# Twelve FFN units over one token half first, score products of step 0 ahead of natural(1), and context keys 2 and 3 expanded in one go

## The chip, the cores and the metric

The kernel runs on one core of one Trainium2 chip. The time is the device time of one execution in microseconds (us), the median of several runs. The core has five engines with queues of their own: TensorE (PE in the profile), VectorE (DVE), ScalarE (ACT), GpSimd (POOL) and SyncE (SP), which here only issues DMA. Each engine works its list of instructions in order and waits on semaphores.

## The reference

One transformer layer on x of 4 batches x 256 tokens x 128 channels, with a context of 4 x 64 tokens x 64 channels:

```python
h  = layernorm(x)
q, k, v  = heads(h @ Wq + bq), heads(h @ Wk + bk), heads(h @ Wv + bv)   # 16 heads of 8
qc = heads(h @ Wcq + bcq);  kc, vc = heads(ctx @ Wck + bck), heads(ctx @ Wcv + bcv)
y  = softmax(causal(q k^T / sqrt(8))) v + softmax(qc kc^T / sqrt(8)) vc
x1 = x + y @ Wp + bp
h2 = layernorm(x1)
aff = sigmoid(h2 @ Wr + br)                  # 32 experts; the top 8, scaled to sum 1, give w_full
shared = (silu(h2 @ Wg_s + bg_s) * (h2 @ Wu_s + bu_s)) @ Wd_s + bd_s
down_e = (silu(h2 @ Wg[e] + bg[e]) * (h2 @ Wu[e] + bu[e])) @ Wd[e] + bd[e]   # inner size 64
out = x1 + shared + sum_e w_full[:, e] * down_e
```

All 32 experts are computed for all 1,024 tokens and weighted afterwards.

## The kernel before

**Precision.** Nearly every operand x is held as a rounded half `x_hi` and a rest `x_lo = x - x_hi`, and a product is three matmuls: hi*hi, hi*lo, lo*hi (`product3`, lines 1341 to 1343). ACT makes the rounded half, DVE or POOL the rest, so each product has two small steps on other engines in front of it.

**Attention.** 16 steps (`STEPS`), step i being batch i // 4 and head group i % 4 (4 heads). PE's loop (line 1603) does in step i: the first two score products (`scores(i, 0)`, `scores(i, 1)`), the transposes of the row maxima of step i+1 (`turn_max`), the natural scores of step i+2 for those maxima (`natural`, with `turn_out(i - 2)` inside), the last two score products (`scores(i, 2)`, `scores(i, 3)`), whatever `tail_at[i]` lists, then the value products of step i-1 (`attend_self`, `attend_context`), then `late_at[i]`. DVE builds key blocks (`expand`), takes the maxima (`maxima`) and divides the outputs (`normalize`); ACT places the maxima (`shift`), takes exponentials (`exps`), rounds and copies (`copy_out`); POOL applies the causal selection to probs, builds context key blocks of groups 2 and 3 (`expand_ctx`, line 592), adds self and context outputs (`add_y`) and makes the rests of FFN weights (`split_unit`, line 626). In step 0 PE also does `natural(1)` before the loop and `context_values` between the score products.

**The tail of a batch.** When the 4 steps of a batch are done: `y_turn` (transpose), `project` (product with Wp; DVE adds x, takes `stats`; POOL raises to the power -0.5; DVE `norm`), `x2_turn` (transpose), `router` (product with Wr; ACT sigmoid or Silu; DVE `top`, `weights`), `route_turn` (transpose). Each goes through PSUM bank 7 (`B_MISC`), and `take_misc` makes PE wait until the one before has been read. For batches 0 and 1 these lie between attention steps (`tail_at`, `late_at`, `between_at`), for batches 2 and 3 partly beside the FFN: the tables `pe_beside`, `act_beside`, `v_beside` (lines 334 to 358) say at which item n and in which of three places (A, B, C) each engine takes them.

**FFN.** 17 units (`UNITS`): 16 pairs of experts, and the shared one. Tokens come in two halves of 512 (`CHUNK`); half 0 is batches 0 and 1, half 1 is batches 2 and 3. One item is one unit over one half; `WORK` (line 53) lists the 34 items: the first `LEAD` = 6 units over half 0, the same 6 over half 1, then units one by one over both halves, and the last 4 units over half 0 and then half 1. Item n on PE: gate (3 matmuls), place A, up (3), place B, wide (1, the routing weights spread over rows, `spread_routes`), down of item n-2 (3), place C. ACT takes Silu of gate and rounds hid, DVE computes `gated` and `hid`, and the rest `hid_lo` is made by POOL for the items in `POOL_LO` (0 to 7 and 31) and by DVE for the others. The first gate over half 1 is item 6 and needs `x2_turn` of batch 3; its wide needs `route_turn` of batch 3. Attention and FFN share PSUM banks: wide 1 waits for `normalized` 15 (line 1664).

**Weights.** SP loads each unit into one of 6 slots (`load_unit`), a load of unit u waits until POOL has made the rest of unit u-6. ACT rounds (`round_unit`, line 799), for units from 6 on after item `SPLIT_AT` and after PE's last down of the unit that had the slot, since rounded half and rest have 6 slots too.

## Time and profile before

| | us |
|---|---|
| median of 3 runs | 215.67 |
| the three runs | 212.80, 215.67, 219.47 |
| the profiled execution | 214.26 |
| its span, first to last instruction | 212.5 |
| PE busy | 192.5 (91%) |
| DVE busy | 161.1 (76%) |
| ACT busy | 136.0 (64%) |
| POOL busy | 95.7 (45%) |

The profiled execution took 214.26 us, 1.76 more than its span. The page gives the busy time of each engine, the busy share and the clock granted to TensorE in 40 slices, the chain of work that ended last (70% PE, 12% DVE, 6% issue, 5% ACT, 3% POOL), and the costliest groups of instructions. Times below are from the start of the span. In rows of the timeline the bracket at the end is the idle time of the engine before the instruction and what released it.

### The profile page before, as it was taken

What the parts mean: (1) busy time and instruction counts of PE and PEld (TensorE: products, weight loads), DVE (VectorE), ACT (ScalarE), POOL (GpSimd) and SP (SyncE); (2) the same over time, 40 slices, a digit from 0 to 9 for tenths busy, and PEclk for the clock granted to TensorE, in tenths of its full rate; (3) what the DMA queues carried; (4) which work ended last, traced back from release to release, by engine and by line L of the source; (5) the groups of instructions that cost most, each with busy time, mean ns of one, the idle gap of its engine ahead of it and who ended that gap; (6) DMA issues with size and microseconds to landing.
All of it is one profiled execution on the core that took longest, in us unless ns stands there. A gap on an engine that the chain in (4) does not pass through costs nothing.

```text
span 212.5 us, 4008 instructions
## 1 busy us (share of the span) xinstructions
PE 192.5 (91%) x1249; PEld 140.5 (66%) x1249; DVE 161.1 (76%) x379; ACT 136.0 (64%) x272; POOL 95.7 (45%) x150
## 2 busy tenths in 40 slices
PE   7967979999999996999797886949999999999993
PEld 2635757777777674777565664737888888887662
DVE  2989997676788869985731689776778888887882
ACT  4456778787898886897735444424577566555571
POOL 7799782142644766277342152516254332220020
PEclk9999999999999999999958999999999999999999
DMA  4365423232333242103101010000033000000003
GB/s 114 87 150 141 108 65 79 55 81 71 93 96 79 69 103 57 37 0 77 37 3 37 0 37 2 0 0 3 0 75 78 19 2 0 0 0 0 5 0 99
DMA packets 20434, 10.40 MB, mean 49 GB/s; under 512 B 11881, under 2 KB 18542, under 8 KB 20414
## 3 DMA queue, kind: packets, MB, share of 16 engines
q1 hardware_dynamic: 19290, 9.24, 17.6%
q0 software_dynamic: 672, 0.69, 1.4%
q10 hardware_dynamic: 452, 0.23, 0.5%
q8 instruction: 10, 0.16, 0.3%
q14 instruction: 10, 0.08, 0.1%
HBM read 4.51 MB, written 0.52 MB: 24 GB/s over the span
## 4 chain that ended last, share of the span: by engine, by line
PE 70%; DVE 12%; issue 6%; ACT 5%; POOL 3%; DMA 1%; POOLq 1%; DVEq 0%; ACTq 0%
PE psum L1341 12%; PE psum L1342 11%; PE psum L1343 10%; PE psum L1444 5%; PE psum L1535 4%; PE psum L1523 4%; PE psum L1500 4%; PE psum L1443 3%; PE psum L1547 3%; PE psum L1667 3%; PE psum L1505 3%; PE psum L1466 2%; PE psum L1528 2%; PE psum L1509 2%; PE psum L1486 1%
## 5 line engine op out<-in xcount | busy, mean ns | idle before, releaser
L913 ACT ACTIVATE gate<-psum,bias_cols 128x512 f32<-128x512 f32 (+2 forms) x35 | 23.5, 675 | 28.7 <-PE psum L1343 28.6
L790 ACT ACTIVATE probs<-psum 128x512 f32<-128x512 f32 x64 | 36.4, 597 | 7.3 <-PE psum L1505 3.4
L1285 DVE SCALAR_TENSOR_TENSOR gated<-psum,bias_cols,gate 128x512 f32<-128x512 f32 x32 | 24.0, 750 | 11.5 <-ACT gate L913 11.5
L629 POOL TENSOR_TENSOR w_ffn_lo<-w_ffn,w_ffn_hi 128x384 fp32r<-128x384 f32 x17 | 20.6, 1212 | 26.7 <-ACT w_ffn_hi L804 26.0
L1341 PE MATMUL psum<-xT_hi,w_ffn_hi 128*128 128x512 f32 x66 | 26.9, 407 | 0.0
L1342 PE MATMUL psum<-xT_lo,w_ffn_hi 128*128 128x512 f32 x66 | 26.1, 396 | 0.0
L1343 PE MATMUL psum<-xT_hi,w_ffn_lo 128*128 128x512 f32 x66 | 26.0, 393 | 0.0
L1444 PE MATMUL psum<-key_blocks,query_rows 96*128 96x512 f32 x48 | 24.1, 544 | 0.0
L699 POOL TENSOR_TENSOR hid_lo<-hid,hid_hi 128x512 fp32r<-128x512 f32 x9 | 11.6, 1291 | 25.9 <-ACT hid_hi L922 25.1
L1297 DVE TENSOR_TENSOR hid<-gated,psum 128x512 f32<-128x512 f32 x32 | 21.8, 682 | 1.6 <-PE psum L1667 1.1
L922 ACT CAST hid_hi<-hid 128x512 fp32r<-128x512 f32 (+1 forms) x33 | 20.2, 613 | 3.8 <-DVE hid L1297 3.1
L654 POOL TENSOR_SCALAR_AFFINE_SELECT probs<-probs 128x512 f32<-128x512 f32 x16 | 10.3, 643 | 22.9 <-ACT probs L790 22.9
L1080 DVE TENSOR_REDUCE row_max<-psum 128x4 fp32r<-128x1024 f32 x16 | 19.5, 1216 | 0.0
L962 DVE TENSOR_TENSOR hid_lo<-hid,hid_hi 128x512 fp32r<-128x512 f32 (+2 forms) x26 | 17.2, 663 | 1.1 <-ACT hid_hi L922 0.9
L797 ACT COPY o_sb<-psum 128x512 f32<-128x512 f32 x16 | 9.4, 586 | 11.7 <-PE psum L1535 11.7
L658 POOL TENSOR_SCALAR_AFFINE_SELECT probs<-probs 128x512 f32<-128x512 f32 x16 | 10.2, 637 | 14.2 <-ACT probs L790 14.2
L1076 DVE TENSOR_REDUCE row_max<-psum 128x4 fp32r<-128x512 f32 x16 | 11.0, 689 | 6.8 <-PE psum L1444 6.8
L1443 PE MATMUL psum<-causal,ident_bf 128*128 128x512 bf16 x32 | 12.5, 389 | 3.4 <-DVE key_blocks L982 1.7
L728 ACT ACTIVATE key_blocks<-key_rows,head_mask 100x256 fp32r<-100x256 f32 x32 | 14.4, 498 | 1.3 <-DMA key_rows<-keys 1.3
L1341 PE MATMUL psum<-hid_hi,w_ffn_hi 128*128 128x512 f32 (+2 forms) x35 | 14.4, 411 | 0.4 <-POOL hid_lo L699 0.3
L1343 PEld LDWEIGHTS psum<-xT_hi,w_ffn_lo 128*128 128x128 f32 x66 | 12.5, 189 | 3.1
L1341 PEld LDWEIGHTS psum<-xT_hi,w_ffn_hi 128*128 128x128 f32 x66 | 12.4, 188 | 3.1 <-issue 0.6
(184 smaller groups left out, 476.5 us busy)
## 6 DMA issues: line engine op xcount, KB each, us to landing
query_rows<-queries SPq DMA_DIRECT2D x46, 64.0 KB, 2.1
key_rows<-keys SPq DMA_DIRECT2D x39, 32.0 KB, 1.9
w_ffn<-in_L_ffn_Wg SPq DMA_DIRECT2D x16, 64.0 KB, 1.9
w_ffn<-in_L_ffn_Wu SPq DMA_DIRECT2D x16, 64.0 KB, 2.2
w_ffn<-in_L_ffn_Wd SPq DMA_DIRECT2D x16, 64.0 KB, 2.1
ckey_rows<-ckeys POOLq DMA_DIRECT2D x12, 32.0 KB, 1.9
key_rows<-keys POOLq DMA_DIRECT2D x9, 32.0 KB, 1.8
x_sb<-in_x SPq DMA_DIRECT2D x2, 128.0 KB, 2.6
```

The lines of the kernel that those rows point to most:

```text
L629: ins = pool.tensor_tensor(w_ffn_lo[:, k, :, :], w_ffn[:, k, :, :], w_ffn_hi[:, k, :, :].bitcast(F32), ALU.subtract).then_inc(ffn_lo, 1)
L790: act.activation(probs[:, i % 2, c, :], bank(B_ST + c % 2), ACT.Exp, scale=SCALE).then_inc(exp_done, 1)
L913: act.activation(gate[rows_of(n), n % 3, part], psum[of, B_GATE + n % 2, part], ACT.Silu, bias=bias_cols[of, BIAS_GATE + u:BIAS_GATE + u + ...
L922: act.copy(hid_hi[rows_of(n - 1), (n - 1) % 3, :], hid[rows_of(n - 1), (n - 1) % 3, :]).then_inc(hid_rounded, 1)
L1080: dve.tensor_reduce(to[:, 1, :], psum[:, B_NAT1:B_NAT1 + 2, :].rearrange("p k (j c) -> p j k c", j=GROUP), AX.XY, ALU.max).then_inc(max_do ...
L1285: dve.scalar_tensor_tensor(out=gated[:, n % 3, :], in0=bank(B_UP + n % 2), scalar=bias_cols[:, BIAS_UP + u:BIAS_UP + u + 1], in1=gate[:, n ...
L1297: dve.tensor_tensor(hid[:, n % 3, :], gated[:, n % 3, :], bank(B_WIDE + n % 2), ALU.mult).then_inc(hid_done, 1)
L1341: pe.matmul(dst, w_hi, x_hi, start=start, stop=False, skip_group_check=True)
L1342: pe.matmul(dst, w_hi, x_lo, start=False, stop=False, skip_group_check=True)
L1343: return pe.matmul(dst, w_lo, x_hi, start=False, stop=stop, skip_group_check=True)
L1443: pe.matmul(to, ident_bf[:, :], causal[:, :, :], start=True, stop=False, skip_group_check=True)
L1444: return pe.matmul(to, query_rows[0:KR, b % 2, g, 0, P * q:P * (q + 1)], blocks[:, :, P * k:P * (k + 1)], start=not diagonal, stop=True, s ...
```

## The change

1. `LEAD` is 12: twelve units go over half 0, then the same twelve over half 1. `POOL_LO` becomes items 0 to 11 and 31. The number of matmuls does not change.
2. Units 6 to 16 get places of their own for the rounded half and the rest (`w_late_hi`, `w_late_lo`), so rounding no longer waits for a down; ACT rounds them after items 2 to 7, 14, 16, 18, 20 and 22 (`ROUND_AT`), and POOL splits units 6 to 11 between its `lower_half` calls.
3. The tail of batches 2 and 3 is laid out anew over items 0 to 10. `x2_turn(2)` leaves step 15 for item 0; `attend(15)` and `turn_out(14)` go behind up of item 0, `turn_out(15)` behind up of item 1. `route_turn(1)` is now ahead of the FFN on ACT too.
4. The transposed outputs of steps 12 to 15 go to banks 0, 1, 3 and 6 instead of the shared bank 7 or 5, with waits on `normalized` in front of gate 0, gate 1 and up 1.
5. In steps 13 to 15 DVE puts the sigmoid rest of `router(1)` behind `y_turn(2)`, and `weights(1)` behind `normalize(12)`; in step 15 PE does `turn_out(13)` ahead of `attend(14)`. POOL takes the power of batch 2 after its loop.
6. Step 0: PE does `scores(0, 0)` and `scores(0, 1)` ahead of `natural(1)`, and `scores(0, 2)`, `scores(0, 3)` ahead of `turn_max(1)`; ACT and DVE are reordered to suit; POOL expands context keys 2 and 3 in one go, ahead of the first selection.

```diff
-LEAD = 6
+LEAD = 12
-SPLIT_AT = {LAST_USE[u - SLOTS] + 4: u for u in range(SLOTS, UNITS)}
+ROUND_AT = {n: u for n, u in zip((2, 3, 4, 5, 6, 7, 14, 16, 18, 20, 22), range(SLOTS, UNITS))}
...
+        w_late_hi = sb("w_late_hi", [P, UNITS - SLOTS, 3, P], F32R)
+        w_late_lo = sb("w_late_lo", [P, UNITS - SLOTS, 3, P], F32R)
...
-        between_at[STEPS - 1] = [("norm", 2)]
-        tail_at[STEPS - 1] = [("x2_turn", 2), ("route_turn", 1)]
+        tail_at[STEPS - 1] = [("route_turn", 1)]
+        pe_beside = {(0, "B"): [("attend", STEPS - 1), ("turn_out", STEPS - 2)],
+                     (0, "C"): [("x2_turn", 2)],
+                     (1, "B"): [("turn_out", STEPS - 1)],
+                     (1, "C"): [("router", 2)],
+                     (2, "C"): [("y_turn", 3)],
+                     (3, "C"): [("project", 3)],
+                     (5, "C"): [("route_turn", 2), ("x2_turn", 3)],
+                     (6, "C"): [("router", 3)],
+                     (LEAD - 2, "B"): [("route_turn", 3)]}
+        act_beside = {(0, "B"): [("x2_turn", 2)],
+                      (2, "B"): [("router", 2)],
+                      (3, "A"): [("y_turn", 3)],
+                      (5, "C"): [("route_turn", 2), ("x2_turn", 3)],
+                      (7, "B"): [("router", 3)],
+                      (LEAD - 2, "B"): [("route_turn", 3)]}
+        v_beside = {(0, "C"): [("turn_out", STEPS - 2), ("x2_turn", 2)],
+                    (1, "C"): [("turn_out", STEPS - 1), ("router", 2)],
+                    (2, "C"): [("top", 2)],
+                    (3, "A"): [("y_turn", 3)],
+                    (3, "C"): [("project", 3), ("stats", 3)],
+                    (4, "A"): [("weights", 2)],
+                    (4, "C"): [("norm", 3)],
+                    (6, "A"): [("x2_turn", 3)],
+                    (6, "C"): [("router", 3)],
+                    (7, "C"): [("top", 3)],
+                    (8, "C"): [("weights", 3)]}
+        RSTD_ITEM = 4
-        POOL_LO = [*range(8), LAST_ITEM - 2]
+        POOL_LO = [*range(LEAD), LAST_ITEM - 2]
...
-            return {STEPS - 2: B_ST + 1, STEPS - 1: B_OUT}.get(i, B_MISC)
+            return {STEPS - 4: B_NAT0, STEPS - 3: B_NATC, STEPS - 2: B_NAT1 + 1, STEPS - 1: B_OUT}.get(i, B_MISC)
...
             expand_ctx(2)
-            pool.wait_ge(pool_ckey_blocks_set, GROUP)
+            expand_ctx(3)
+            pool.wait_ge(pool_ckey_blocks_set, 2 * GROUP)
...
+            tail("project", 2)
+            split_unit(SLOTS - 1)
             add_y(STEPS - 2)
-            add_y(STEPS - 1)
-            split_unit(SLOTS - 1)
...
                 if n == RSTD_ITEM:
                     tail("project", BATCH - 1)
+                if n == 1:
+                    add_y(STEPS - 1)
                 lower_half(n)
-            for u in range(SLOTS, UNITS):
+                if n + 1 in ROUND_AT:
+                    split_unit(ROUND_AT[n + 1])
+            for u in range(LEAD, UNITS):
                 split_unit(u)
...
-                if u >= SLOTS:
-                    act.wait_ge(m_down, LAST_USE[u - SLOTS] + 1)
-                act.copy(w_ffn_hi[:, k, :, :], w_ffn[:, k, :, :]).then_inc(ffn_rounded, 1)
+                act.copy(hi_of(u), w_ffn[:, k, :, :]).then_inc(ffn_rounded, 1)
...
+            exps(0, (0, 1))
             expand(2)
+            act.wait_ge(have_neg_mean, 1)
+            norm(4)
+            norm(5)
+            exps(0, (2, 3))
+            shift(1)
+            norm(6)
+            norm(7)
...
             expand_ctx(1)
+            expand(2)
             maxima(1)
-            expand(2)
             cvalues()
...
             turn_max(0)
-            natural(1)
             for i in range(STEPS):
...
                 scores(i, 0)
                 scores(i, 1)
                 if i == 0:
+                    natural(1)
                     context_values()
+                    scores(0, 2)
+                    scores(0, 3)
...
                 pe.wait_ge(ffn_lo, u + 1)
+                if n < 2:
+                    pe.wait_ge(normalized, STEPS - 3 + n)
...
+                        if n == 1:
+                            pe.wait_ge(normalized, STEPS - 1)
```

## Rows read from the trace of the kernel before

**Rows 1.** Busy time by stretch: each engine's us and instructions, granted clock, DMA
```profile
142.00:200.00 58.00, 58.00 (x250) 46.24 (x250) 45.66 (x70) 34.63 (x62) 18.47 (x14) 1.00 0.07 16
```
**Rows 2.** Timeline of PE, 101 to 142 us, instructions behind a stall
```profile
103.75 0.63 PE L1547 MATMUL psum<-ident,o_sb 128*128 128x128 f32 x4 [0.43 <-DVE yT_lo L962]
...
105.96 0.33 PE L1341 MATMUL psum<-w_qkv_hi,yT_hi 128*128 128x128 f32 x1 [0.90 <-DVE o_norm L1115]
...
114.40 0.44 PE L1596 MATMUL psum<-ident,route 128*128 128x128 f32 x2 [1.10 <-DVE xT_lo L962]
...
118.41 0.28 PE L1341 MATMUL psum<-w_r_hi,xT_hi 128*128 128x32 f32 x1 [0.95 <-ACT routeT L824]
...
126.32 0.30 PE L1341 MATMUL psum<-w_qkv_hi,yT_hi 128*128 128x128 f32 x1 [0.74 <-DVE yT_lo L962]
...
132.52 0.41 PE L1584 MATMUL psum<-ident,x_norm 128*128 128x128 f32 x2 [1.39 <-DVE x_norm L1183]
...
141.84 0.41 PE L1596 MATMUL psum<-ident,route 128*128 128x128 f32 x2 [2.70 <-DVE route L1203]
```
**Rows 3.** Busy time by stretch: where the granted clock is low
```profile
106.00:113.40 7.40, 7.30 (x42) 5.03 (x42) 2.48 (x10) 2.94 (x6) 2.97 (x6) 0.54 0.09 19
```
**Rows 4.** Timeline of PE in steps 0 and 1, behind a stall
```profile
20.08 0.38 PE L1443 MATMUL psum<-causal,ident_bf 128*128 128x512 bf16 x1 [1.40 <-issue]
...
30.33 0.50 PE L1466 MATMUL psum<-ckey_blocks,query_rows 96*128 96x256 f32 x2 [1.07 <-POOL ckey_blocks L597]
```
**Rows 5.** Timelines of POOL and DVE, 22 to 31 us
```profile
27.85 2.42 POOL L597 TENSOR_TENSOR ckey_blocks<-ckey_rows,head_mask 100x256 fp32r<-100x256 f32 x4
...
23.07 1.24 DVE L982 TENSOR_SCALAR key_blocks<-key_rows,head_mask 100x256 fp32r<-100x256 f32 x2
...
26.98 1.22 DVE L1080 TENSOR_REDUCE row_max<-psum 128x4 fp32r<-128x1024 f32 x1
```
**Rows 6.** Busy time by stretch: gate 0, attend(15), turn_out(14); and two score products
```profile
114.60:117.25 2.65, 2.65 (x29) 1.38 (x28) 0.00 (x0) 1.12 (x3) 0.00 (x0) 1.00 0.00 0
104.14:104.95 0.81, 0.81 (x9) 0.72 (x6) 0.71 (x3) 0.08 (x2) 0.30 (x1) 1.00 0.00 0
```
**Rows 7.** Timeline of ACT, 104 to 118 us
```profile
104.87 1.08 ACT L790 ACTIVATE probs<-psum 128x512 f32<-128x512 f32 x2 [0.73 <-PE psum L1505]
...
108.87 0.51 ACT L804 CAST w_ffn_hi<-w_ffn 128x384 fp32r<-128x384 f32 x1
...
113.90 1.28 ACT L898 ACT_TABLE_LOAD   x1
...
117.40 0.69 ACT L913 ACTIVATE gate<-psum,bias_cols 128x512 f32<-128x512 f32 x1
```
**Rows 8.** The page's costliest groups: count, busy us and mean ns, idle before
```profile
L1285 DVE SCALAR_TENSOR_TENSOR gated<-psum,bias_cols,gate 128x512 f32<-128x512 f32 x32 | 24.0, 750 | 11.5 <-ACT gate L913 11.5
...
L1297 DVE TENSOR_TENSOR hid<-gated,psum 128x512 f32<-128x512 f32 x32 | 21.8, 682 | 1.6 <-PE psum L1667 1.1
L922 ACT CAST hid_hi<-hid 128x512 fp32r<-128x512 f32 (+1 forms) x33 | 20.2, 613 | 3.8 <-DVE hid L1297 3.1
...
L797 ACT COPY o_sb<-psum 128x512 f32<-128x512 f32 x16 | 9.4, 586 | 11.7 <-PE psum L1535 11.7
```
**Rows 9.** Groups of instructions on POOL, 142 to 200 us, same columns
```profile
L629 POOL TENSOR_TENSOR w_ffn_lo<-w_ffn,w_ffn_hi 128x384 fp32r<-128x384 f32 x11 | 14.6, 1326 | 26.0 <-ACT w_ffn_hi L804 26.0
L699 POOL TENSOR_TENSOR hid_lo<-hid,hid_hi 128x512 fp32r<-128x512 f32 x3 | 3.9, 1293 | 6.1 <-ACT hid_hi L922 6.1
```
**Rows 10.** Timelines of DVE and POOL, 117 to 132 us
```profile
117.79 0.29 DVE L1115 TENSOR_TENSOR o_norm<-psum,r_den 128x128 f32<-128x128 f32 x1
...
123.34 1.18 DVE L1187 TENSOR_TENSOR affinity<-exp_neg,r_logits 128x64 f32<-128x64 f32 x1
...
131.77 0.60 DVE L1183 TENSOR_SCALAR x_norm<-x,moments,rstd 128x128 f32<-128x128 f32 x2 [0.16 <-POOL rstd L646]
...
131.03 0.71 POOL L646 TENSOR_TENSOR rstd<-var_eps,minus_half 128x2 f32<-128x2 f32 x1 [3.12 <-DVE var_eps L958]
```

More of the change, by code:

```diff
@@ L329, in build @@
         tail_at[STEPS - 2] = [("project", 2)]
-        between_at[STEPS - 1] = [("norm", 2)]
-        tail_at[STEPS - 1] = [("x2_turn", 2), ("route_turn", 1)]
-        pe_beside = {(0, "A"): [("attend", STEPS - 1), ("turn_out", STEPS - 2), ("router", 2)],
-                     (0, "B"): [("turn_out", STEPS - 1)],
-                     (1, "B"): [("y_turn", 3)],
-                     (2, "C"): [("project", 3)],
-                     (3, "C"): [("route_turn", 2)],
-                     (4, "A"): [("x2_turn", 3)],
-                     (4, "C"): [("router", 3)],
-                     (LEAD, "B"): [("route_turn", 3)]}
@@ L915, in _ @@
                 if n == 0:
-                    tail("route_turn", 1)
+                    copy_out(STEPS - 1)
                 left_over(n, "A")
@@ L1228, in _ @@
                     maxima(i + 2, i - 2)
-                else:
-                    if i == STEPS - 2:
-                        long_part("weights", 1)
-                    for name, b in between_at.get(i, ()):
-                        long_part(name, b)
-                    normalize(i - 2)
+                if i == STEPS - 2:
+                    tail_rest("router", 1)
+                    normalize(i - 2)
+                    long_part("weights", 1)
+                if i == STEPS - 1:
+                    normalize(i - 2)
+                    long_part("norm", 2)
+                    break
                 for name, b in tail_at.get(i, ()):
```

87 lines of the change are left out of this document (32 added, 55 removed).

## The prediction

> **What bounds the kernel now.** I read the page's engine totals first: PE is busy for 91% of the span and has 70% of the chain that ended last, so the question is where PE does not work, or works slowly. Then the busy time by stretch. From 142 to 200 us PE is never idle and issues 250 matmuls in 58.0 us [rows 1]: 0.232 us each, 2.32 us for an item of ten. DVE has 45.7 us there, ACT 34.6, POOL 18.5. This stretch is bound by the number of matmuls, and the change leaves that number alone. So only what lies ahead of it can move. From 101 to 142 us, the end of attention and the first seven items, the timeline of PE shows eight stalls over 0.4 us [rows 2] (seven stand there; the eighth is 0.45 us, at 130.00): 0.43, 0.90, 1.10, 0.95, 0.74, 0.45, 1.39 and 2.70, in sum 8.66 us. All are waits for DVE or ACT in the tail of batches 2 and 3. The reader should see from the releasers that this is one chain: six items (14 us of PE) are too little cover for what follows attention(15), and the chain's last link, `route_turn(3)`, stands in PE's queue ahead of item 6. The row of the granted clock shows one more loss there: between 106.0 and 113.4 it is 0.54 on average though PE is busy for 7.30 of 7.40 us [rows 3], so most of it ran at 1.2 GHz instead of 2.4. That is (1 - 0.54) x 7.4 = 3.4 us lost, and it follows the stalls of 0.43 and 0.90. At the start, `natural(1)` comes after 1.40 us without work, and `natural(3)` waits 1.07 us for POOL's context keys [rows 4].
>
> **Step 0.** Before, PE waits 1.40 us for key blocks of step 1 while the shift that `scores(0, 0)` needs is nearly there. The two score products now fill that gap, and `natural(1)` starts when it did. The reductions of step 1 start 0.3 us later (DVE now does `expand(2)` first), but the expansion of step 2 that took 1.24 us beside POOL's work is out of their way. What sets `turn_max(2)` is DVE's last reduction of step 2, ending at 28.20 [rows 5]. Walking DVE's list with these durations I get 27.9, since its `expand(3)` now meets POOL and takes the 1.24. That is 0.3 us. POOL's second expansion, 2.42 us starting at 27.85, now follows the first at about 24.8 and ends at 27.2, so `natural(3)` at about 28.3 doesn't wait: 1.07 us more, with its restart 1.2. The selection of step 0 moves from 25.5 to 27.2 and ends at 28.5; its reader `attend(0)` comes at about 31. Key rows and query rows issued by SP are landed well before either order asks. Sum 1.5 us. Bounds: nothing, if DVE's chain sets everything; 2.5, both stalls whole. From 30 to 101 us PE is full but for one wait in step 10 that the change leaves, so I take the gain as lasting.
>
> **Steps 13 to 15.** `turn_out(12)` has a bank of its own, so it no longer waits until `y_turn(2)` is read (0.43). `project(2)` no longer waits for `normalize(12)` (0.90). `x2_turn(2)` leaves the queue, and with it the 1.10 wait of `route_turn(1)`, which now only needs `weights(1)`, long ready. PE has little idle time left there, and I expect the clock to stay at 2.4 GHz: 3.4 us. POOL now takes the rest of unit 4 ahead of the selection of step 15, and waits with it for ACT's rounding; both are done before `attend(15)`, which stands behind gate 0 and up 0. Then the 0.95 behind `routeT` goes, because `router(2)` is an item later.
>
> **A new stall in item 1.** Up 1 writes the bank of `turn_out(14)` and waits for `normalize(14)`, which on DVE stands behind gated 0 and hid 0, and these behind the first Silu. Count from the end of `attend(14)`. PE: two score products 0.81; `route_turn(1)` 0.2; gate 0, `attend(15)`, `turn_out(14)` 2.65 [rows 6]; up 0 0.70; wide 0 0.23; `x2_turn(2)` 0.2; gate 1 0.70: 5.5 us. ACT: copy 0.59 [rows 8], rounding 0.51, two exponentials 1.08, routeT 0.4, table load 1.28 and its dummy 0.2, Silu 0.69 [rows 7]: 4.75; DVE: gated 0.75, hid 0.68 [rows 8], normalize 0.55 (its second half is 0.29, [rows 10]): 6.75. PE waits 1.3 us. The ends are nothing and 2.5 (if the chain starts a microsecond later). Before, the table load lay beside idle PE time. The Trainium skill (ScalarE: Activation LUTs, Terms) says about 2.7 us for a table load, and in its section What ACT_TABLE_LOAD costs about 1.28; the trace agrees with the second, and by the first this stall would be 2.7 us.
>
> **Items 2 to 11.** Now twelve items, 28 us, lie over the tail of batch 3, and every other wait of rows 2 (0.74, 0.45, 1.39, 2.70) belongs to a link which now has at least one item of slack, but one: `x2_turn(3)` behind item 5. From the end of gate 4: ACT Silu 0.69 and hid 0.61 [rows 7, 8]; POOL rest of hid 1.29, the split of unit 8 1.33 [rows 9], the power 0.71, then DVE's norm 0.60 [rows 10]: 5.2, with hand-overs 5.4. PE: up 4, wide, down 2, all of item 5 and `route_turn(2)`: 4.3. A new stall of 1.1 us; nothing to 2.5. `lower_half(4)` waits behind the same norm on POOL, down 4 is read 4.7 us after wide 4 and still in time. Per item POOL now has 1.29 + 1.33 = 2.62 us against PE's 2.32 in the six items with a split: it falls behind by 0.3 each, 1.8 in all, and the two items between hid and down cover that. Rounding costs ACT 0.51 in items where it has over 0.9 free. SP loads units 6 to 10 before the FFN as now; unit 11 is asked for at about 113 and rounded ten microseconds later.
>
> **The sum.** Removed 8.66 + 3.4 = 12.1; added 1.3 + 1.1 = 2.4; step 0 1.5; together 11.2 us. The profiled execution took 214.26 (span 212.5), so 203.1. The median of the three runs is 1.4 higher; I can't see why, part of it is likely a longer stretch at 1.2 GHz, so I carry half over: 203.8.
>
> **The rivals.**
> (a) Forecast: 203.8, its own range 201.5 to 206. Chance 0.60.
> (b) The clock falls again. The 1.3 us stall stands among transposes and value products with few rows or columns, as the 0.43 and 0.90 did before 106 us. Against it: stalls of 1.10 and 0.95 between such work, and 2.70 later, left the clock at 1.00. Price 3.4: 207.2. Chance 0.15.
> (c) DVE or POOL becomes the bound in items 2 to 8. DVE has 2.32 - 1.43 = 0.89 us free an item, 7.1 over eight, and both `top` and `weights` of two batches, which made the wait of 2.70, with stats and norms: some 11 us, as an estimate. It falls 3 to 4 us behind; the slack of up is about two items. And `affinity`, 64 elements, took 1.18 us while POOL made a rest [rows 10]; four such per batch could wait a POOL instruction each, 1.3 us. Then PE waits some 3 us: 206.8. Chance 0.13. The Trainium skill (SBUF — State Buffer, SBUF: two separate sides) says that DVE instructions with two SBUF inputs and POOL's exclude each other for a whole instruction; the trace agrees with that 1.18, and this rule speaks against a change that gives POOL four more rests beside the tail.
> (d) It gives little: the stalls only moved and the waits come back as others of the same chain, since `project(3)`, `x2_turn(3)` and `route_turn(2)` still need DVE in order. Kept: the clock's 3.4 and half of step 0: 211. Against it: 13 more FFN matmuls (3.0 us) now stand ahead of `y_turn(3)`, and five more items between it and `route_turn(3)`. Chance 0.09.
> (e) Slower. All of items 0 to 11 now hang on POOL's `hid_lo`. If POOL's 1.29 were stretched by DVE's lock, PE would run at POOL's pace. To eat 11 us in twelve items, POOL has to take 3.3 us an item; for slower by 2%, 3.7: 220. Rows 9 have 1.29 beside a DVE at 79%. Chance 0.03.
>
> **How the numbers follow.** The low end is the sum without the two new stalls, 200.7; the high end adds the clock (3.4), the whole 1.4 of the median and 0.6 of (c): 208.5. Beyond stand (d), (e) and a little of (c). Faster by over 2% (about what a measurement of this kernel can tell from no change) is below 211.4: (a), (b), (c) and half of (d), 0.93. Within 2%: 0.04. Slower: 0.03.
>
> **What would show it.** Right: PE's timeline from the last attention step to item 12 has two stalls over 0.5 us, before up 1 (releaser DVE `o_norm`) and before `x2_turn(3)` (DVE `x_norm`); granted clock 1.00 throughout; `y_turn(3)` at about 118, gate 0 at about 107; `natural(3)` without a wait. Wrong: stalls before downs with POOL `hid_lo` as releaser mean (c) or (e); before ups or wides with DVE `gated` or `hid`, (c); a clock near 0.5 between 105 and 120, (b). The early gain is wrong if PE's `scores(2, 0)` starts later than 33.

## The result, and the profile after

Four executions of the changed kernel took 204.82, 204.88, 205.11 and 206.95 us, median 205.0; the kernel before had a median of 215.1 beside them. The ratio is 0.9585, with a 95% interval of 0.9477 to 0.9693. (The ratios here and below leave out executions of over 1.5% above the fastest of the same kernel.) The prediction was 203.8, in a range of 200.5 to 208.5. The profiled execution took 204.82 (span 203.1), against 214.26 (span 212.5) before.

The timeline of PE after the change, the instructions behind a stall of over 0.2 us from 84 us to the end of the tail (start, us, engine, line, operation, then the idle time before it and its releaser; line numbers are 8 to 20 higher than before):

```profile
112.27 0.50 PE L1356 MATMUL psum<-xT_hi,w_ffn_hi 128*128 128x512 f32 x1 [1.01 <-DVE o_norm L1127]
...
120.15 0.30 PE L1356 MATMUL psum<-w_qkv_hi,yT_hi 128*128 128x128 f32 x1 [0.24 <-DVE yT_lo L974]
...
126.06 0.41 PE L1611 MATMUL psum<-ident,route 128*128 128x128 f32 x2 [0.35 <-DVE route L1215]
...
128.37 0.44 PE L1599 MATMUL psum<-ident,x_norm 128*128 128x128 f32 x2 [1.91 <-ACT routeT L834]
...
140.89 0.41 PE L1611 MATMUL psum<-ident,route 128*128 128x128 f32 x2 [0.74 <-DVE route L1215]
...
144.30 0.50 PE L1356 MATMUL psum<-hid_hi,w_late_hi 128*128 128x512 f32 x1 [0.47 <-POOL hid_lo L707]
```

These answer [rows 2]. They are up 1, `project(3)`, `route_turn(2)`, `x2_turn(3)`, `route_turn(3)` and down 9, and in sum 4.72 us where before there were 8.66. The prediction had two of them, 2.4 in sum.

Busy time by stretch after the change (us, then busy us and instruction count of PE, its weight load, DVE, ACT and POOL; the granted clock; DMA share and GB/s):

```profile
105.00:113.40 8.40, 7.39 (x60) 4.81 (x55) 4.50 (x14) 6.42 (x13) 5.30 (x8) 1.00 0.19 47
112.00:130.00 18.00, 15.22 (x74) 11.99 (x75) 15.90 (x41) 8.47 (x18) 10.93 (x12) 1.00 0.17 42
130.00:145.00 15.00, 13.79 (x63) 10.76 (x63) 13.38 (x29) 8.21 (x16) 9.70 (x9) 1.00 0.08 20
```

The first row answers [rows 3]: where the clock was 0.54 it is 1.00. The other two show who is full: DVE is busy for 29.3 of the 33 us from 112 to 145, 89%, and POOL for 20.6.

Steps 0 to 2 in PE's timeline, and the same queue at gate 0 and at `y_turn(3)`:

```profile
19.35 0.74 PE L1515 MATMUL psum<-query_rows,key_blocks 100*128 100x256 f32 x4 [0.76 <-DVE queries L1033]
20.00 0.38 PE L1458 MATMUL psum<-causal,ident_bf 128*128 128x512 bf16 x1
...
28.28 0.40 PE L1481 MATMUL psum<-ckey_blocks,query_rows 96*128 96x256 f32 x2
...
32.05 0.73 PE L1515 MATMUL psum<-query_rows,key_blocks 100*128 100x256 f32 x4
...
106.54 0.48 PE L1356 MATMUL psum<-xT_hi,w_ffn_hi 128*128 128x512 f32 x1
...
117.20 0.38 PE L1586 MATMUL psum<-ident,y_nat 128*128 128x128 f32 x2
```

`natural(1)` at 20.00 and the context part of `natural(3)` at 28.28 have no wait any more, against 1.40 and 1.07 in [rows 4]. Not all of the first gap is filled: `scores(0, 0)`, now ahead of `natural(1)`, waits 0.76 us for DVE. A wait of 0.30 at 24.40 in the kernel before is gone too, so the waits from 18 to 31 us fell from 2.77 to 0.76, by 2.0. `scores(2, 0)` starts at 32.05 (34.18 before), gate 0 at 106.54 (114.60 before), `y_turn(3)` at 117.20 (122.16 before).

**The clock, execution by execution.** Each execution comes with its mean granted clock, and the times go with it in steps. Executions of the two kernels, on the chips of these runs:

```
mean clock   kernel before, us        kernel after, us
0.997-0.999  none in 43               204.8, 204.9, 204.9, 205.0, 205.1
0.992        212.9 to 213.1           none
0.982-0.984  214.0 to 214.6           206.4, 206.5, 207.0
0.974-0.975  215.7 to 216.2           none
0.967        216.4 to 216.9           none
0.959        217.6 to 217.8           none
0.952        218.9 to 219.4           none
0.944        220.1 to 220.4           none
```

From 212.9 to 220.3 there are six steps, 1.2 us each on average. The kernel before was never seen at full clock; one step below 212.9 would be 211.7, an estimate, and an almost equal kernel (experiment 3) took 211.64 at 0.998. That gives 211.6. A second estimate comes from experiment 2, the kernel before with two banks changed, whose profiled execution was at 1.00 throughout. The first line of its page:

```profile
PE 189.3 (91%) x1249; PEld 138.5 (66%) x1249; DVE 161.3 (77%) x379; ACT 136.2 (65%) x272; POOL 95.9 (46%) x150
```

Its span was 208.5, so PE idled 19.2 us, 0.8 less than the 20.0 of the kernel before; 210.23 and 0.8 are 211.1. Profile to profile, the 9.4 us are then 2.7 to 3.2 for the clock and 6.2 to 6.7 at equal clock. The pages of the two kernels split them in another way: PE's idle time fell from 20.0 to 14.3 us, its busy time from 192.5 to 188.8, 5.7 and 3.7.

### The profile page after: what moved, and what is told of

Read it like the earlier page. It is cut to its first block, busy times and chain, and to the rows that moved or that the text cites. A ratio compares the mean times of both kernels' runs of the same rounds, so it can differ in the third digit from the quotient of the medians.

```text
span 203.1 us, 3982 instructions
## 1 busy us (share of the span) xinstructions
PE 188.8 (93%) x1237; PEld 138.5 (68%) x1249; DVE 162.2 (80%) x375; ACT 135.7 (67%) x272; POOL 98.1 (48%) x154
## 4 chain that ended last, share of the span: by engine, by line
PE 65%; DVE 18%; issue 6%; ACT 5%; POOL 3%; DMA 1%; DVEq 0%; POOLq 0%
PE psum L1356 10%; PE psum L1358 9%; PE psum L1357 9%; PE psum L1459 6%; PE psum L1515 5%; PE psum L1550 4%; PE psum L1538 4%; PE psum L1520 3%; PE psum L1562 3%; DVE gated L1300 2%; POOL hid_lo L707 2%; PE psum L1458 2%; PE psum L1687 2%; PE psum L1524 2%; PE psum L1543 2%
## 5 line engine op out<-in xcount | busy, mean ns | idle before, releaser
L707 POOL TENSOR_TENSOR hid_lo<-hid,hid_hi 128x512 fp32r<-128x512 f32 x13 | 16.8, 1291 | 32.9 <-ACT hid_hi L934 30.6
L638 POOL TENSOR_TENSOR w_late_lo<-w_ffn,w_late_hi 128x384 fp32r<-128x384 f32 x11 | 12.2, 1112 | 18.7 <-ACT w_late_hi L814 18.7
L1356 PE MATMUL psum<-xT_hi,w_late_hi 128*128 128x512 f32 x42 | 17.0, 404 | 0.0
L1358 PE MATMUL psum<-xT_hi,w_late_lo 128*128 128x512 f32 x42 | 16.6, 394 | 0.0
L1357 PE MATMUL psum<-xT_lo,w_late_hi 128*128 128x512 f32 x42 | 16.5, 392 | 0.0
L974 DVE TENSOR_TENSOR hid_lo<-hid,hid_hi 128x512 fp32r<-128x512 f32 (+2 forms) x22 | 15.2, 696 | 1.1 <-ACT hid_hi L934 0.9
L1687 PE MATMUL psum<-routeT,spread 128*128 128x512 f32 x32 | 12.8, 401 | 0.0
L1515 PE MATMUL psum<-query_rows,key_blocks 100*128 100x256 f32 x64 | 11.9, 307 | 0.8 <-DVE queries L1033 0.8
L1515 PEld LDWEIGHTS psum<-query_rows,key_blocks 100*128 100x128 f32 x64 | 8.6, 189 | 5.6 <-issue 4.4
L994 DVE TENSOR_SCALAR key_blocks<-key_rows,head_mask 100x256 fp32r<-100x256 f32 x32 | 11.9, 415 | 0.0
## 6 DMA issues: line engine op xcount, KB each, us to landing
x_sb<-in_x SPq DMA_DIRECT2D x2, 128.0 KB, 2.7
```

Of the source, the lines that this page charges most:

```text
L707: pool.tensor_tensor(hid_lo[:, n % 3, :], hid[:, n % 3, :], hid_hi[:, n % 3, :].bitcast(F32), ALU.subtract).then_inc(pool_lo_done, 1)
L1356: pe.matmul(dst, w_hi, x_hi, start=start, stop=False, skip_group_check=True)
L1357: pe.matmul(dst, w_hi, x_lo, start=False, stop=False, skip_group_check=True)
L1358: return pe.matmul(dst, w_lo, x_hi, start=False, stop=stop, skip_group_check=True)
L1515: ins = pe.matmul(psum[:, to, SEQ * j:SEQ * (j + 1)], key_blocks[0:ROWS, i % RING, 2 * c + j, 0:P], query_rows[0:ROWS, b % 2, g, 0, :], st ...
```

## The experiments

**1. How much step 0 gives, and whether it lasts.** The changed kernel with steps 0 to 2 and the spread of the context keys as before.

```diff
-            pool.wait_ge(pool_ckey_blocks_set, GROUP)
+            expand_ctx(3)
+            pool.wait_ge(pool_ckey_blocks_set, 2 * GROUP)
...
-            natural(1)
...
+                    natural(1)
...
+                    scores(0, 2)
+                    scores(0, 3)
```

(Here a plus is the changed kernel, which is undone; ACT's and DVE's lists go back with it.)

> The changed kernel with step 0 as in the kernel before: natural(1) ahead of the loop, the last two score products of step 0 behind natural(2), context keys 3 expanded behind the selections of step 0. Everything behind step 1 stays changed. In the two traces PE reaches scores(2, 0) 2.1 us earlier and y_turn(1) of step 10 still 2.1 us earlier after the change. Theory: the gain of step 0 lasts to the end, so this kernel takes 205.0 + 2.1 = 207.1 us and its PE stalls in the FFN stay at 4.7 us. Rival: the tail of the attention gives it back, 205.0 to 205.5. My prediction's term was 1.5 us.

Executions: 207.14 and 207.15 (clock 0.998, 0.991), 208.34 and 208.46 (0.990, 0.989); ratio to before 0.971 [0.965, 0.977]. PE's timeline of that kernel:

```profile
20.05 0.38 PE L1453 MATMUL psum<-causal,ident_bf 128*128 128x512 bf16 x1 [1.39 <-issue]
...
30.30 0.50 PE L1476 MATMUL psum<-ckey_blocks,query_rows 96*128 96x256 f32 x2 [1.07 <-POOL ckey_blocks L606]
...
132.04 0.44 PE L1594 MATMUL psum<-ident,x_norm 128*128 128x128 f32 x2 [1.90 <-ACT routeT L835]
```

Both early waits are back (and the 0.3 at 24.38) and every later wait over 0.3 us has the length that it has in the changed kernel (1.90 for 1.91, 0.74 for 0.74). At full clock it takes 207.1 against 204.9 to 205.0. So step 0 is worth 2.1 to 2.2 us, all of it reaches the end, and it doesn't touch the tail.

**2. The first two waits alone.** The kernel before, with a bank of its own for `turn_out` in steps 12 and 13.

```diff
-            return {STEPS - 2: B_ST + 1, STEPS - 1: B_OUT}.get(i, B_MISC)
+            return {STEPS - 4: B_NAT0, STEPS - 3: B_NATC, STEPS - 2: B_ST + 1, STEPS - 1: B_OUT}.get(i, B_MISC)
...
+                if n < 2:
+                    pe.wait_ge(normalized, STEPS - 3 + n)
```

> The kernel before, with one part of the change alone: the transposed outputs of steps 12 and 13 go to banks 0 and 1, with the waits this needs ahead of gate 0 and gate 1. Takes away what makes PE wait 0.43 us ahead of turn_out(12) and 0.90 us ahead of project(2). Theory (the clock fell because PE was idle there): the granted clock stays at 1.00 between 105 and 115 us, and the time falls by 1.3 for the waits and 3.4 for the clock, 215.1 to 210.4 us. Rival (the clock falls by itself in this stretch, where the work is transposes and value products): only 1.3 us, 213.8, with a stretch near 0.5 in the trace. Second rival: the waits come back at x2_turn(2) and route_turn(1), and nothing is gained.

Executions: 210.23 (1.0), 211.84 and 212.01 (0.991, 0.992), 214.62 (0.976); ratio 0.988 [0.980, 0.996]. PE's timeline in place of the first two rows of [rows 2]:

```profile
109.26 0.41 PE L1584 MATMUL psum<-ident,x_norm 128*128 128x128 f32 x2 [0.55 <-DVE x_norm L1183]
...
110.59 0.44 PE L1596 MATMUL psum<-ident,route 128*128 128x128 f32 x2 [0.92 <-DVE xT_lo L962]
```

The waits of 0.43 and 0.90 are gone, and 0.55 of a new one has come before `x2_turn(2)`. `route_turn(1)` waits 0.92 for 1.10, so the waits fell by 1.0 in all. At the same clock (0.991 to 0.992) this kernel takes 211.9 where the one before takes 212.9, which is that 1.0. Its median gained 2.6 against before; the rest came with the clock, which was 1.00 throughout in its profile. That execution fits the theory's 210.4; in the other three the clock fell all the same, so the two waits are not the only cause.

**3. The clock alone.** The kernel before, with four idle matmuls of the kernel's own kind ahead of `project(2)`. They add work that nothing reads and fill most of the wait of 0.90.

```diff
+                if i == STEPS - 2:
+                    run_idle(4, B_NAT0)
```

> The kernel before with four more matmuls of 512 columns into bank 0, which nothing reads, between the last score product of step 14 and project(2): 0.93 us of PE work where PE waits 0.90 us. No wait and no order of the rest is changed. Theory (idle time let the clock fall): granted clock 1.00 from 106 to 113 us, time lower by 3.4, about 211.7 us. Rival (the kind of work lets it fall, or the 0.43 alone is enough): clock 0.5 as before, time equal or up to 0.2 longer, 215.

Ten executions: 211.64 (0.998), 212.74 (0.992), three of 214.2 to 214.6 (0.984), 215.67 (0.976), four of 216.7 to 216.9 (0.967); ratio 0.999 [0.992, 1.006]. Busy time by stretch in its profile:

```profile
105.00:113.40 8.40, 7.14 (x68) 4.23 (x65) 3.61 (x15) 5.84 (x11) 4.10 (x7) 1.00 0.11 25
...
138.00:145.00 7.00, 5.94 (x20) 4.80 (x21) 3.60 (x8) 2.09 (x4) 2.58 (x2) 0.76 0.00 0
```

The clock held where the wait was filled, and fell behind the later wait of 2.69 (`route_turn(3)`), whose like of 2.70 in the profile of the kernel before had left it at 1.00. So the idea that this one gap makes the clock fall doesn't hold over many executions: with it filled, the clock falls elsewhere, and the median doesn't move.

**4. What POOL's instructions do to DVE's small ones.** The kernel before, with two subtractions of 128x512 on POOL behind `hid_lo(4)`, beside the work that feeds `route_turn(3)`. They are added work that nothing reads.

```diff
+                if n == 4:
+                    for k in range(2):
+                        pool.tensor_tensor(dump[:, k, :], x_sb[:, 0:4, :].rearrange("p t c -> p (t c)"),
+                                           x_sb[:, 4:8, :].rearrange("p t c -> p (t c)"), ALU.subtract)
```

> The kernel before with two more subtractions on POOL behind the rest of hid 4, 128x512, both inputs in SBUF, into a tile that nothing reads. They run at about 139 to 141.5 us, where POOL is idle and DVE does top(3) and weights(3), which took 1.36 us from 140.25 on. POOL's next work comes at 143. Theory (DVE's small instructions wait for a POOL instruction): weights(3) takes 1.2 to 2.5 us longer, some of its instructions measure about 1 us instead of 0.2, and the stall of PE ahead of route_turn(3), 2.70 us, becomes 4 to 5. Rival (1.18 us for affinity and the like come from something else, such as the Silu beside it): weights(3) stays at 1.4 us and the stall at 2.7.

Its one execution took 218.48 us at 0.969, a single time from which nothing is read. The timelines of POOL, DVE and PE in it:

```profile
140.74 2.50 POOL L709 TENSOR_TENSOR dump<-x_sb 128x512 f32<-128x512 f32 x2
...
142.34 0.98 DVE L1196 SCALAR_TENSOR_TENSOR affinity<-not_top,affinity 128x64 f32<-128x64 f32 x1
...
144.49 0.41 PE L1601 MATMUL psum<-ident,route 128*128 128x128 f32 x2 [3.42 <-DVE route L1208]
```

The twin of this `affinity` in the kernel before takes 0.23 us beside an idle POOL. Here it takes 0.98 and ends when POOL's pair ends (143.32 and 143.24). PE's wait grows by the same 0.7, from 2.70 to 3.42. The direction is confirmed; the size is less than I expected, since only one of the seven instructions of `weights(3)` fell into POOL's time.

**5. The stall of up 1.** The changed kernel, with DVE's normalization of step 14 ahead of the first gated product.

```diff
-        v_beside = {(0, "C"): [("turn_out", STEPS - 2), ("x2_turn", 2)],
+        v_beside = {(0, "A"): [("turn_out", STEPS - 2)],
+                    (0, "C"): [("x2_turn", 2)],
```

> The changed kernel with DVE's normalize(14) moved from behind hid 0 to ahead of gated 0. In the trace of after, turn_out(14) ended at 109.9 us, DVE waited until 110.18 for the first Silu, and up 1 waited 1.01 us for normalize(14). Theory: that stall goes, since normalize(14) no longer stands behind the Silu and the table load: minus 1.0 us, 204.0. Rival: the item is bound by the Silu anyway, hid 0 is 0.3 us later and the stall comes back as another ahead of up 2, wide 1 or down 0: 205.0.

Executions: 204.46 (0.991), 205.88 (0.983), 207.30 and 207.45 (0.974); ratio 0.959 [0.950, 0.968]. The wait ahead of up 1 is gone, those of 0.20, 0.35, 1.90 and 0.43 are as they were; the 0.74 ahead of `route_turn(3)` is missing as well, which experiment 9 explains by the clock. So the predicted mechanism holds. But the clock fell in all four executions, and the median, 206.6, gains nothing. At the same clock, 205.88 at 0.983 stands against 206.4 to 207.0 of the changed kernel, 0.6 to 1.1 less. In the profile it fell behind the waits at 80.8 (1.63) and at 128.8 (1.90), neither of which this edit touches.

**6. `x2_turn(3)` first.** The changed kernel, with `norm(3)` ahead of `weights(2)` on DVE and `x2_turn(3)` ahead of `route_turn(2)` on PE and ACT.

```diff
-                      (5, "C"): [("route_turn", 2), ("x2_turn", 3)],
+                      (5, "C"): [("x2_turn", 3), ("route_turn", 2)],
...
-                     (4, "A"): [("weights", 2)],
-                     (4, "C"): [("norm", 3)],
+                     (4, "C"): [("norm", 3), ("weights", 2)],
```

> The changed kernel with DVE's norm(3) ahead of weights(2) (weights(2) from ahead of gated 4 to behind norm(3)), and x2_turn(3) ahead of route_turn(2) on PE and ACT. In after, weights(2) took 3.1 us from 122.8 on, and gated 4, hid 4 and norm(3) followed it; PE waited 0.35 + 1.91 us behind item 5. Theory (DVE's queue made norm(3) late): norm(3) comes as soon as POOL's power is done, at 126.0 instead of 127.3, x2_turn(3) waits about 0.4 us, route_turn(2) waits for weights(2), done at about 129, some 1.5 to 2: gain between 0 and 1 us, 204.0 to 205.0, with x2_turn(3) a microsecond earlier. Rival, and what the prediction said (POOL's split of unit 8 sets it): x2_turn(3) isn't earlier.

Executions: 207.62 (0.991), 207.99, 208.35 and 209.06 (0.983); ratio 0.968 [0.961, 0.975]. PE's timeline:

```profile
126.67 0.41 PE L1598 MATMUL psum<-ident,x_norm 128*128 128x128 f32 x2 [1.10 <-DVE x_norm L1194]
...
130.84 0.69 PE L1610 MATMUL psum<-ident,route 128*128 128x128 f32 x2 [3.76 <-DVE xT_lo L973]
```

`x2_turn(3)` comes 1.7 us earlier, and 3.76 us of a new wait follow: `route_turn(2)` takes the same bank, and DVE reads `x2_turn(3)`'s out of it only in slot (6, A). An edit that I hadn't followed to the bank's next reader; what it shows is the first row.

**7. A longer lead.** The changed kernel with thirteen units over the first token half ahead instead of twelve, and unit 12 rounded after item 10.

```diff
-LEAD = 12
+LEAD = 13
-ROUND_AT = {n: u for n, u in zip((2, 3, 4, 5, 6, 7, 14, 16, 18, 20, 22), range(SLOTS, UNITS))}
+ROUND_AT = {n: u for n, u in zip((2, 3, 4, 5, 6, 7, 10, 16, 18, 20, 22), range(SLOTS, UNITS))}
```

> The changed kernel with thirteen units over half 0, so one item more of cover; route_turn(3) is at item 11, unit 12 is rounded after item 10, POOL makes the rests of items 0 to 12. Theory (the chain of batch 3 is still a little longer than its cover; DVE is late by then): the stall of 0.74 us ahead of route_turn(3) and the 0.47 behind it go, those at items 1 to 5 (3.5 us) stay: minus 1.0 us, 204.0. Rival (DVE is the bound over the whole stretch): the stalls move and the time stays 205.0.

Executions: 206.24 to 206.60 (0.991 to 0.983); ratio 0.959 [0.952, 0.966]. The 0.74 ahead of `route_turn(3)` is gone, the 0.45 ahead of down 9 stays, and so do 1.00, 0.36 and 1.91. But this profile was at 0.983, and there the changed kernel hasn't the 0.74 either (experiment 9), so it isn't shown that the edit removed it. At 0.983 it took 206.5 and 206.6 against the changed kernel's 206.4, 206.5 and 207.0: no gain can be told.

**8. Edits 5, 6 and 7 together.**

> The three edits together (normalize(14) ahead of gated 0, norm(3) ahead of weights(2), thirteen units first). Theory: they act on different stalls, the sum is minus 2.0 to 3.0: 202.0 to 203.0. Rival (DVE's whole work in items 0 to 8 is the bound): not below 204.

206.99 (0.992) to 209.20 (0.975); ratio 0.968 [0.960, 0.976]. Its waits are 0.24, 1.08, 3.76 and 0.43: those of experiment 6 without the ones that 5 and 7 remove. The 202.0 to 203.0 were missed by far, through the bank of experiment 6; nothing else can be read from it.

**9. The changed kernel once more,** on the chip and beside the kernels of experiments 10 and 11.

> The changed kernel itself, beside its variants on the same chip. So far four executions: 204.8, 204.9 and 205.1 us at a mean granted clock of 0.997 to 0.999, and 206.95 at 0.983. Variants with the same stalls of 1.91 and 0.35 us behind item 5 had a clock of 0.983 in most executions, with a stretch at half between 127 and 133 us, right behind those stalls. Theory: the clock also falls in this kernel in some executions, each time for 2 to 3 us of time: median 205.0 to 207.0. Rival: the changed kernel keeps its clock, 205.0 in nearly all.

204.92 and 204.99 (0.998), 206.44 and 206.48 (0.982); ratio 0.958 [0.950, 0.966]. The profiled one was at 0.982. Busy time by stretch of it, and `route_turn(3)` in PE's timeline:

```profile
80.00:84.00 4.00, 3.21 (x25) 1.48 (x26) 3.79 (x14) 1.23 (x3) 1.86 (x3) 0.67 0.46 113
...
127.00:133.00 6.00, 3.76 (x12) 2.97 (x13) 3.96 (x9) 3.02 (x7) 2.64 (x4) 0.72 0.16 36
...
142.60 0.39 PE L1611 MATMUL psum<-ident,route 128*128 128x128 f32 x2
```

The same two stretches of the first profile have 1.00 and 1.00. The waits that they follow are the same to 0.01 us in both: 1.65 at step 10, 1.91 ahead of `x2_turn(3)`. One program with the same waits thus kept its clock in one execution and lost it in another; it cost 1.5 us. Other waits are not the same: the 0.24 ahead of `project(3)` is gone, and so is the 0.74 ahead of `route_turn(3)`, where the slower PE comes later. The 0.74 is missing in every profile here with a low clock at 128 to 135 us (experiments 5 to 9). So such a profile can't show that an edit removed it.

**10. DVE's order mended for the bank.** The changed kernel, with `norm(3)` first, then the rest of `x2_turn(3)` in (5, B), `weights(2)` in (5, C), and `route_turn(2)` two items later.

```diff
-                      (5, "C"): [("route_turn", 2), ("x2_turn", 3)],
+                      (5, "C"): [("x2_turn", 3)],
+                      (7, "C"): [("route_turn", 2)],
...
-                     (4, "A"): [("weights", 2)],
-                     (6, "A"): [("x2_turn", 3)],
+                     (5, "B"): [("x2_turn", 3)],
+                     (5, "C"): [("weights", 2)],
```

> The changed kernel with another order on DVE in items 4 to 6: norm(3) right behind hid 4, the rest of x2_turn(3) between gated 5 and hid 5, and weights(2) only behind hid 5; route_turn(2), which needs weights(2), goes behind item 7 on PE and ahead of item 8's rounding on ACT. In after, norm(3) came at 127.31 us though POOL's power ended at 126.0, because weights(2) (3.1 us), gated 4 and hid 4 were ahead of it. Theory (DVE's queue, stretched by POOL's instructions, is what made x2_turn(3) late): the stalls of 0.35 and 1.91 us become one of 1.1 or less ahead of x2_turn(3), router(3) doesn't wait, and the clock no longer falls at 127 to 133 us: 1.2 to 2 us less than after at the same clock, 203.0 to 203.8. Rival (my prediction's: POOL's queue with the split of unit 8 sets norm(3)): x2_turn(3) at most 0.3 us earlier, 204.8. Second rival (DVE's whole work is the bound): the stall comes back ahead of an up, a wide or route_turn(3).

Executions: 204.97 to 205.24 (0.997 to 1.0, four), 206.49 and 206.69 (0.989, 0.988); ratio 0.957 [0.950, 0.965]. DVE's and PE's timelines:

```profile
126.08 0.60 DVE L1197 TENSOR_SCALAR x_norm<-x,moments,rstd 128x128 f32<-128x128 f32 x2 [1.69 <-POOL rstd L657]
...
126.83 0.41 PE L1601 MATMUL psum<-ident,x_norm 128*128 128x128 f32 x2 [1.09 <-DVE x_norm L1197]
...
133.66 0.44 PE L1613 MATMUL psum<-ident,route 128*128 128x128 f32 x2 [1.11 <-DVE logits L1158]
...
141.29 0.41 PE L1613 MATMUL psum<-ident,route 128*128 128x128 f32 x2 [0.83 <-DVE route L1217]
```

`x2_turn(3)` starts 1.5 us earlier, with DVE now idle for 1.69 until POOL's power is done. But the time at full clock is 205.0 as before: 1.11 has come ahead of `route_turn(2)` (its releaser is `logits`, DVE's reading of the bank), and the sum of the waits is 4.68 instead of 4.72. The forecast 203.0 to 203.8 was missed; the second rival held.

**11. Orders 10 and 5 together.** The diff is the two above.

> The order of e_order and normalize(14) ahead of gated 0. Each takes a stall of its own; the one ahead of up 1 (1.01 us) was gone in the trace of e_norm14. Theory: minus 1.0 for the one and 1.2 to 2 for the other, with a clock of 0.99 or more: 202.0 to 202.8 us. Rival: DVE is the bound over items 0 to 8, the sum isn't reached and the time stays above 203.5.

204.10, 204.12 and 204.17 (0.999, 1.0, 1.0), 205.41 to 205.74 (0.992 to 0.987); ratio 0.954 [0.947, 0.960]. The wait of up 1 is gone, the others stand (0.20, 1.09, 1.12, 0.83, 0.47). At full clock it is 0.8 us below the changed kernel (204.1 for 204.9) and 0.9 below experiment 10, from which it differs by this one edit: the 1.01 of up 1, nearly whole. The sum of the two gains wasn't reached, as the rival had it.

**12. Everything with slack.** As 11, with `route_turn(2)` at item 8 and `LEAD` 13.

> As e_both (normalize(14) ahead of gated 0, norm(3) and the rest of x2_turn(3) ahead of weights(2)), with route_turn(2) one place later (item 8, place B) and thirteen units over half 0, so that route_turn(3) is at item 11. e_both took 204.1 us in its three executions at a granted clock of 0.999 or more, with stalls of PE of 0.20, 1.09, 1.12 (ahead of route_turn(2)), 0.83 (ahead of route_turn(3)) and 0.47 us. Theory: DVE is late in items 6 to 9, and PE waits for it only where a link stands in PE's queue; with both links moved back the 1.12 and 0.83 go: 202.2 us at full clock. Rival (DVE's work, with its waits for POOL, is the bound up to item 10, wherever the links stand): ups, wides or downs wait instead, 203.5 to 204.1.

204.04 to 204.29 (1.0, three), 205.31 to 205.65 (0.992 to 0.987); ratio 0.950 [0.944, 0.955]. PE's timeline, in place of its last two links:

```profile
135.88 0.50 PE L1359 MATMUL psum<-hid_hi,w_late_hi 128*128 128x512 f32 x1 [1.16 <-POOL hid_lo L710]
...
145.01 0.50 PE L1359 MATMUL psum<-hid_hi,w_late_hi 128*128 128x512 f32 x1 [0.98 <-POOL hid_lo L710]
```

No link waits any more behind `x2_turn(3)`; the downs wait instead (3.6 us of PE's idle time from 100 to 150 us for 3.7), and at full clock the time is that of experiment 11, not the 202.2 of the theory. Its profile was at 0.987, with the low stretch at 80 to 88 us, ahead of all this. The releaser named is POOL, but POOL itself had idled 2.5 us ahead of each of these two `hid_lo`, for ACT's rounding, and that for DVE's hid. DVE's timeline has no idle time from 128.0 to 144.4 us, which is the tail of both batches:

```profile
129.90 1.25 DVE L1210 TENSOR_TENSOR affinity<-affinity,r_top 128x64 f32<-128x64 f32 x1
131.18 0.91 DVE L1217 CAST route<-affinity 128x64 fp32r<-128x64 f32 x1
...
140.05 1.16 DVE L1217 CAST route<-affinity 128x64 fp32r<-128x64 f32 x1
```

In `weights(2)` and `weights(3)` these three take 3.32 us where the same instructions take 0.22, 0.20 and 0.20 in the kernel before, beside an idle POOL: 2.7 us of DVE's time are waits. This and 11 are the fastest kernels of the study, 0.4% below the changed one at full clock.

## Why the prediction was right, and where it was not

**Sign and size.** Forecast 203.8, measured 205.0. Its sum was made against the profiled execution and came to 203.1; the profiled one after took 204.82, 1.7 more. The 0.7 that it added for the median hid part of this, and by luck: the medians of before and after lie 0.8 and 0.2 above their profiled executions. Two errors offset each other besides, step 0 put too low and the tail too high. By its terms:

```
                     predicted   measured
step 0                  1.5      2.1 to 2.2 (experiment 1)
waits of the tail       6.3      3.9 in the timelines
clock                   3.4      2.7 to 3.2, estimates; 3.7 is what PE's busy time fell by
together               11.2      9.4, as profile to profile
```

Of the 6.2 to 6.7 at equal clock 4.1 to 4.6 are left once step 0 (2.1) is taken off. That is 0.2 to 0.7 above the timelines' 3.9, by which estimate of the clock one takes; no run settles it.

**Step 0: right, too small.** The gap before `natural(1)` is filled but for 0.76 us, and `natural(3)` no longer waits for POOL, at 28.28 as worked out (about 28.3). The gain at `turn_max(2)` was put at 0.3 on the ground that `expand(3)` would now meet POOL and take 1.24 us; it took 0.97, and `turn_max(2)` came 0.67 earlier (27.57 for 28.24). The mark set for it, `scores(2, 0)` no later than 33, was met with 32.05. That the gain lasts was an assumption; experiment 1 shows it.

**Steps 13 to 15: right.** No wait over 0.2 us from 81 to 111 us, gate 0 at 106.5 (predicted 107), `y_turn(3)` at 117.2 (118), a clock of 1.00 there. The term for the clock was the step closest to a guess: its size is about right (3.4 for 2.7 to 3.2), its cause isn't shown. No execution of the kernel before was at 0.997 or above in 43, and five of eight after the change were; but with one wait filled (experiment 3) one of ten was, and with the first two waits of [rows 2] removed (experiment 2) one of four.

**Item 1: right.** The stall ahead of up 1 came with the releaser that was named, 1.01 us for 1.3. The table load took its 1.28 there, with no gap on either side. Experiments 5 and 11 show the mechanism: moving DVE's `normalize(14)` removes the stall and gives back 0.8 to 0.9 us.

**Items 2 to 11: wrong by 2.6 us, and this is the step that failed.** One wait of 1.1 was predicted here; there are five, 3.71 in sum. Part of it stands as worked out: POOL's chain (rest of hid, split, power) does end late. When DVE has nothing else ahead of the norm (experiment 10), PE waits 1.09, and DVE's releaser is POOL's power. Only the split's duration was taken wrongly, 1.02 us in the trace for the 1.33 of [rows 9]: that was measured beside DVE's own `hid_lo`, which items 0 to 11 don't have (last section). In the changed kernel the wait is 0.8 longer and waits of 0.24, 0.35, 0.74 and 0.47 stand around it. These come from DVE, which the forecast gave no term: the releaser is DVE in the first three, and ahead of down 9 POOL waits for ACT's rounding and ACT for DVE's hid. DVE's timeline and POOL's after the change:

```profile
122.78 0.16 DVE L1202 TENSOR_REDUCE top_sum<-top 128x2 f32<-128x16 f32 x1
...
123.12 1.27 DVE L1205 TENSOR_SCALAR top_sum<-top_sum 128x2 f32<-128x2 f32 x1
124.43 0.17 DVE L1206 RECIPROCAL r_top<-top_sum 128x2 f32<-128x2 f32 x1
124.63 0.79 DVE L1207 TENSOR_TENSOR affinity<-affinity,r_top 128x64 f32<-128x64 f32 x1
...
125.83 0.75 DVE L1300 SCALAR_TENSOR_TENSOR gated<-psum,bias_cols,gate 128x512 f32<-128x512 f32 x1
...
127.31 0.60 DVE L1195 TENSOR_SCALAR x_norm<-x,moments,rstd 128x128 f32<-128x128 f32 x2
...
138.67 0.16 DVE L1205 TENSOR_SCALAR top_sum<-top_sum 128x2 f32<-128x2 f32 x1
...
139.32 1.16 DVE L1214 CAST route<-affinity 128x64 fp32r<-128x64 f32 x1
...
123.07 1.30 POOL L707 TENSOR_TENSOR hid_lo<-hid,hid_hi 128x512 fp32r<-128x512 f32 x1 [0.93 <-ACT hid_hi L934]
124.33 1.01 POOL L638 TENSOR_TENSOR w_late_lo<-w_ffn,w_late_hi 128x384 fp32r<-128x384 f32 x1
125.30 0.71 POOL L655 TENSOR_TENSOR rstd<-var_eps,minus_half 128x2 f32<-128x2 f32 x1
...
139.14 1.29 POOL L707 TENSOR_TENSOR hid_lo<-hid,hid_hi 128x512 fp32r<-128x512 f32 x1 [1.74 <-ACT hid_hi L934]
```

`weights(2)` takes 3.1 us. Two of its instructions hold 2.06 of that, and each ends with a POOL instruction: 124.39 and 124.37, 125.42 and 125.34. Their twins beside an idle POOL take 0.16 and 0.23. Not every one waits: the `RECIPROCAL` at 124.43 took 0.17 inside POOL's split, as it does beside an idle POOL. So gated 4, whose gate came out of ACT at 122.49, starts at 125.83; hid 4 is late, ACT's rounding of it waits for it (2.62 us idle), and `routeT`, which stands behind that rounding, is out at 128.3. `x2_turn(3)` takes the bank that `routeT` is copied from. Its own input, `x_norm`, stands behind the same hid 4 on DVE and is out at 127.9; so the bank set the last 0.4 of the 1.91, DVE's norm the rest. ACT's part of it:

```profile
121.80 0.69 ACT L925 ACTIVATE gate<-psum,bias_cols 128x512 f32<-128x512 f32 x1 [1.59 <-PE psum L1358]
...
127.43 0.62 ACT L934 CAST hid_hi<-hid 128x512 fp32r<-128x512 f32 x1 [2.62 <-DVE hid L1312]
127.95 0.37 ACT L834 CAST routeT<-psum 128x256 fp32r<-128x256 f32 x1
```

The bank and ACT's place in it had no term in the forecast.

**Rival (c) was partly right.** It named this mechanism (small DVE instructions that wait for POOL's) and put 3 us on it with a chance of 0.13; measured above the forecast are 2.6. The forecast's own count had DVE 3 to 4 us behind over eight items (11 us of work for 7.1 free) and trusted in the two items of slack that an up has; but the links of the batches stand in PE's queue with less, and they waited. The signs it set for this rival, waits ahead of ups, wides or downs, showed only in the 0.47. Experiments 10 and 12 show that DVE's queue is the bound there: whatever link is given slack, the sum of the waits stays (4.72, then 4.68), or the waits move to the downs. How much of it is DVE's waits for POOL, and not its own work, is read from the durations (2.7 us in experiment 12); no run took POOL's work away. The Trainium skill (SBUF — State Buffer, SBUF: two separate sides) has the pair of ports held by whoever starts first, for a whole instruction. The trace agrees, by the ends above, by the 0.98 of experiment 4 and, the other way round, by the last section. It was quoted in the prediction for two-input instructions; here a TENSOR_SCALAR on 128x2 and a CAST on 128x64 are hit as hard, which may be that section's other case, an instruction in a two-port mode; in which mode they ran no trace shows.

**Rival (b), the clock, in part.** Three of eight executions of the changed kernel lose clock, and 1.5 to 2 us with it, against an expected 3.4; and in the one that was profiled not behind the new stall of 1.01 but behind step 10 (1.65) and `x2_turn(3)` (1.91). **(d)** is excluded by 205.0 against 211. **(e)**: POOL's `hid_lo` kept its 1.29 us (eleven of them in 110 to 146 us, mean 1.291); it was DVE that was held up, not POOL. DVE has no `hid_lo` of its own in these items; where it has, POOL is held up too (last section).

**Still open.** What decides in one execution whether the clock falls behind a wait. Experiment 9 shows waits of 1.65 and 1.91 with both outcomes, experiment 3 that filling one wait is not enough. What the twelve units alone give: no run had the rest of the change with `LEAD` at 6, and the part of the later waits is read from the timelines. Whether the 1.09 ahead of `x2_turn(3)` would go without the split on POOL was argued from the timelines and not tried.

## What to carry to other kernels

Before work is laid over a tail to hide its waits, sum up the second engine too, with what it loses to the engine that it shares ports with: here each of POOL's instructions could add about a microsecond to a DVE instruction of 0.2. Once that engine is the bound, giving a link more slack only moves the wait; read the sum of the waits, not the one that went. And compare kernels at equal granted clock: of 10 us between the medians between 3 and 4 were clock, and variants that differ by half a microsecond are told apart in no other way.
